# Loading the shifted tiles of a step in one transfer per tile over 128 partitions, in place of one per partition quadrant

## What is computed

```python
B, M, D = (2048, 32, 16)
e = jnp.stack([tbl_0[ids[:, 0]], ..., tbl_31[ids[:, 31]]], axis=1)   # x0: (B, 32, 16)
xk = x0
outs = []
for W in (W0, W1, W2):           # (32, 32, 64), (32, 64, 64), (32, 64, 64)
    xk = jax.nn.relu(jnp.einsum('bmd,bhd,mhk->bkd', x0, xk, W))
    outs.append(jnp.sum(xk, axis=2))
z = jnp.concatenate(outs, axis=1)                  # (B, 192)
h = jnp.concatenate([z, dense_ctx], axis=1)        # (B, 208)
h = jnp.maximum(h @ W_top1 + b_top1, 0.0)
h = jnp.maximum(h @ W_top2 + b_top2, 0.0)
y = h @ W_top3
```

## Time and profile before

| | |
|---|---|
| median of 3 runs | 1177.02 us |
| the profiled execution itself | 1183.16 us |
| its span, first to last instruction | 1181.4 us |
| mean granted TensorE clock | 0.993 |
| PE busy | 1126.9 us, 95% |
| DVE busy | 1119.0 us, 95% |
| POOL busy | 914.9 us, 77% |
| ACT busy | 822.8 us, 70% |
| DMA moved | 167.31 MB, mean 142 GB/s |
| queue 1 (SP's) | 59,248 packets, 157.76 MB, 61.3% of 16 engines |

### The profile page before, as it was taken

The page is one execution under the profiler, slowest core; times in us unless marked ns, Lnnn a source line. Parts: engine busy times, 40 slices in busy tenths (PEclk is TensorE's granted clock), DMA queues, the critical chain, the costliest instruction groups (busy, mean ns, idle before and its releaser), DMA issues.

```text
span 1181.4 us, 15688 instructions
## 1 busy us (share of the span) xinstructions
PE 1126.9 (95%) x5370; PEld 399.8 (34%) x5370; DVE 1119.0 (95%) x511; ACT 822.8 (70%) x2259; POOL 914.9 (77%) x639
## 2 busy tenths in 40 slices
PE   0778899999999999999999999999999999999998
PEld 0222223333333333333333333333333333333344
DVE  1689999999999999999999999999999999999995
ACT  0345466776869677686967768696776869678674
POOL 6766888888888888888888888888888888885400
PEclk9998999999999999999999999999999999999999
DMA  6786588666677866657886666688666678866300
GB/s 145 194 197 137 114 173 171 142 145 140 132 150 165 174 141 148 131 123 161 169 173 144 139 131 147 140 171 173 141 142 132 140 145 173 173 139 136 70 1 1
DMA packets 78336, 167.31 MB, mean 142 GB/s; under 512 B 22097, under 2 KB 39905, under 8 KB 78257
## 3 DMA queue, kind: packets, MB, share of 16 engines
q1 hardware_dynamic: 59248, 157.76, 61.3%
q0 software_dynamic: 16384, 4.23, 3.7%
q10 hardware_dynamic: 2624, 4.34, 1.4%
HBM read 157.86 MB, written 8.40 MB: 141 GB/s over the span
## 4 chain that ended last, share of the span: by engine, by line
PE 84%; POOL 4%; DMA 4%; DVE 3%; issue 3%; ACT 1%; ACTq 0%; SPq 0%; DVEq 0%; POOLq 0%
PE acc L758 79%; POOL x_rows L346 3%; PE acc L862 3%; DVE p_dve L653 2%; PE acc L848 1%; POOL p_l L359 1%; PE acc L850 1%; DMA spread<-x_of_steps 1%; DMA q_tile<-x_of_steps 1%; DMA x_of_steps<-x_rows 1%; PE acc L870 1%; DMA x_rows<-in_table,ids_s 0%; ACT xb L411 0%; POOL p_pool L370 0%; DVE z L680 0%
## 5 line engine op out<-in xcount | busy, mean ns | idle before, releaser
L758 PE MATMUL acc<-p_dve,w_s 128*64 128x512 f32 x3840 | 855.8, 595 | 13.9 <-DVE p_dve L653 13.7
L346 POOL DMA_INDIRECT x_rows<-in_table,ids_s x512 | 493.8, 964 | 146.1 <-issue 130.7
L653 DVE TENSOR_TENSOR p_dve<-spread,xb 128x3072 f32<-128x3072 f32 (+2 forms) x225 | 566.1, 2572 | 4.3 <-PE acc L758 2.9
L653 DVE TENSOR_TENSOR p_dve<-spread,xa 128x2048 f32<-128x2048 f32 (+1 forms) x192 | 495.4, 2634 | 9.3 <-PE acc L758 4.1
L758 PEld LDWEIGHTS acc<-p_dve,w_s 128*64 128x64 f32 x3840 | 271.3, 137 | 549.7 <-issue 486.5
L411 ACT ACTIVATE xb<-acc 32x512 f32<-32x512 f32 x512 | 288.8, 564 | 36.1 <-DVE p_dve L653 29.6
L359 POOL TENSOR_TENSOR p_l<-spread,q_tile 128x2048 f32<-128x2048 f32 x59 | 268.4, 4576 | 8.3 <-DMA q_tile<-x_of_steps 7.2
L402 ACT ACTIVATE xa<-acc 64x512 f32<-64x512 f32 x256 | 145.9, 570 | 168.5 <-PE acc L758 126.7
L370 POOL TENSOR_TENSOR p_pool<-spread,x_s 128x1024 f32<-128x1024 f32 x64 | 152.5, 2383 | 95.3 <-PE acc L758 52.8
L419 ACT ACTIVATE x_s<-acc 64x512 f32<-64x512 f32 x256 | 151.5, 592 | 9.2 <-ACT y_row L565 4.7
L758 PE MATMUL acc<-p_l,w_s 32*64 32x512 f32 (+1 forms) x600 | 144.2, 617 | 5.5 <-DVE p_l L706 3.2
(11 more groups left out here) (26 smaller groups left out, 246.2 us busy)
## 6 DMA issues: line engine op xcount, KB each, us to landing
spread<-x_of_steps SPq DMA_DIRECT2D x244, 512.0 KB, 16.9
q_tile<-x_of_steps SPq DMA_DIRECT2D x120, 128.0 KB
x_rows<-in_table,ids_s POOLq DMA_INDIRECT x512, 4.2
x_of_steps<-x_rows SPq DMA_DIRECT2D x60, 128.0 KB
spread<-x_of_steps ACTq DMA_DIRECT2D x4, 512.0 KB, 12.0
spread<-x_of_steps SPq DMA_DIRECT2D x6, 256.0 KB, 4.7
w_s<-in_w SPq DMA_DIRECT2D x2, 512.0 KB, 6.3
spread<-x_of_steps SPq DMA_DIRECT2D x8, 128.0 KB, 3.3
```

The source lines that it names most:

```text
L346: nc.gpsimd.indirect_dma_start(out=x_rows[:, s % 2, i * DIM:(i + 1) * DIM], out_offset=None, in_=table, in_offset=bass.IndirectOffsetOnAxi ...
L653: nc.vector.tensor_tensor(p_dve[:, to:to + n, :], spread[:, s % 3, tile:tile + n, :], over(x[:], n), ALU.mult).then_inc(dve_made, n)
L758: last = nc.tensor.matmul(halves(acc[b * K:(b + 1) * K, :]), w, of_block(prod, b), start=start, stop=stop)
```

## The change

`load_tiles_by` gets a second way, taken when all four quadrants are asked for, that is in `load_a` and `load_b` from step 2 on. It issues one transfer per tile, whose destination is all 128 partitions of that tile and whose source is a pattern of 4 x 32 x 1024: the outer dimension steps by one row (the four quadrants' shifts), the middle one by one row too (the 32 rows).

```diff
         def load_tiles_by(engine, s, first_tile, n, quads, signal):
 
+            if len(quads) == Q:
+
+                for i in range(first_tile, first_tile + n):
+                    first = scratch[s, Q * i + 1:Q * i + 2, :]
+                    src = bass.AP(first.tensor, first.offset, [[COLS, Q], [COLS, FIELDS], [1, COLS]])
+                    engine.dma_start(spread[:, s % 3, i, :], src).then_inc(signal, 16)
+                return
             for q in quads:
                 o = Q * first_tile + q + 1
                 first = scratch[s, o:o + 1, :]
```

## The result

The changed kernel takes 1600.53 us (median of four runs, 1599.1 to 1601.56), the kernel before 1177.66 in the same comparison: a ratio of 1.358, 95% interval 1.355 to 1.361. It is slower, by the mechanism forecast, but by 423 us and not by 956.

A forecast was written before the change was run, and what follows sets the result against it. PE's compute bound the kernel at 34.5 us a step; the DMA queue would become the bound. 78.8 + 61.2, plus 29 periods of 66.7, plus 62.6 gave 2137 of span; + 1.8 - 6.1 gave 2133 us, range 1520 to 2780.

The forecast's parts named there:

- Four engines: The 240 changed `spread` loads: each on 4 engines of 16, queue 1's packets falling by 2880; 85 in 100.
- The price of a tile on four engines: Each changed a or b load: 7.65 us a tile at 17.1 GB/s an engine, 61.2 us for eight.
- the middle row: Profile window 31 to 41 us, two queues writing all quadrants: 274 GB/s, 17.1 an engine, taken for the tile price.
- the fast end: First instants of the a loads, 401 GB/s: 25.1 GB/s an engine, 5.23 us a tile, 1551 us in all.
- The q loads, 2.2 us, and the gap, 3.3 us: Each step: unchanged q loads, plus an unhidden gap from the last b packet to the next a packet.
- The end, 62.6 us after the last b load: Step 31: compute left after b(31) lands, from the group with chunk 4 to the span's end, 62.6 us.
- The gather no longer is waited for: SP's queue each step: the gather wait vanishes, POOL's 28.6 us of work being far below the 66.7 us period.
- rival 3: Changed loads on 8 engines or a like middle: 3.83 us a tile, 36.1 a step, about 1215 us; 3 in 100.
- the 26.6 us of SP's idle time: SP's gather wait each step, 26.6 us, taken to hide any longer issue of the new loads.
- Rival 1: Changed loads on all 16 engines at the fast rate: 5.2 us saved early, 1172 us; 8 in 100.
- SP's issues at nothing: SP's queue: four new issues may take up to 1 us more, hidden by SP's idle time, so no cost.
- The clock: PE idle over 30 us each step: lower clock costed at nothing within steps, some us allowed in the last 62.6.

The follow-up runs named there:

- e1: Changed kernel with the 240 loads' source written 16 x 8 x 1024 in place of 4 x 32 x 1024: 1216.52 us, ratio 1.0015 to the kernel before.
- e2: Changed kernel with the loads' source written 8 x 16 x 1024 in place of 4 x 32 x 1024: 1397.0 us, ratio 1.151 to the kernel before.
- t1: Changed kernel with source 16 x 8 rows, reading other embedding table rows for each load instead of the stored rows: 1181.27 us, ratio 1.002.
- t4: Changed kernel, source still 4 x 32 rows, reading embedding table rows (four engines' rows 33 apart) instead of the stored rows: 1603.68 us, ratio 1.363.
- e4: Changed kernel with one transfer per tile and quadrant, source 4 x 8 rows, 960 transfers of 128 KB: 1577.21 us, ratio 1.299.
- e6: Changed kernel with the last four gathers of a step moved ahead of the products in POOL's queue: 1593.55 us, ratio 1.352.
- e8: The e2 kernel with the last four gathers of a step moved ahead of the products in POOL's queue: 1276.83 us, +98 us.
- t3: Changed kernel with source one run of 128 successive embedding table rows per load, to 128 partitions: 1177.61 us, ratio 1.000.
- e3: Changed kernel with only the a loads in the new form, the b loads by quadrants as before: 1736.95 us, ratio 1.429.
- e5: Changed kernel unedited, run again beside e6 and e8: 1597.33 us against 1179.17 for the kernel before.

## Why the prediction was right in kind and wrong in size

- **Four engines.** Right, and shown by e1 and e2: 56,368 packets against "about 56,370". That the smaller outermost count, here the source's, decides, which I chose without a row for it, holds for 4, 8 and 16. The rule of the Trainium skill ("DMA: Bandwidth & Descriptors", the section on why a DMA increments its semaphore by 16) gives the same three numbers.
- **The price of a tile on four engines, 7.65 us at 17.1 GB/s an engine.** This is the step that failed. Measured are 26 GB/s an engine, 5.0 us a tile, in the whole b set and most of the a set, and 74 GB/s for four, some 18 an engine, only in the first 8 us. I took the middle row since in it all quadrants are written at once; but it has 16 engines in them, and with four the lower rate gives way to the higher. t1 and t4 rule out the re-reading of the same rows as the reason of the lower rate, and e4 shows the start without it; why it lies at the destination is argued above and not shown. Eight tiles so take some 45 us (a from 758 to about 784, b some 20) in place of 61.2. The measured rate is close to the fast end that I had in hand, 5.23 us a tile and 1551 us: the right row was in the prediction and I chose another. With 48.8 us for the period in my own sum in place of 66.7, 29 x 17.9 = 519 us go, and 16 more for step 2's own tiles: 2133 - 535 = 1598, against 1600.53 measured. This puts in the measured period, so it tests the start and the end of the sum and not the price of a step. That the transfers alone give that period is what e6 shows: with the loop broken, the time stays within 4 us.
- **The q loads, 2.2 us, and the gap, 3.3 us.** Nearly right in sum: about 2 us more on the four engines (82 GB/s from 784 to 786), and some 4 us from 805, where the b rows end, to 809, where the a rows begin. What I did not see is that q is now complete only behind the a rows, which is what POOL waits for.
- **The end, 62.6 us after the last b load.** It fits: the stores of step 31 are at 1484.38, the last b rows move at 95 GB/s up to 1534, and from 1534 to 1536 there are 2 GB/s. So b(31) lands at about 1534, 64 us before 1598.0.
- **"The gather no longer is waited for."** Wrong, and the second step that failed: SP waits for it 17.9 us a step. I counted POOL's work and not what it waits for. In the change this is nearly hidden by the b loads (e6: 4 us). It is what made rival 3 wrong, whose 36.1 us a step would be +38 us: eight engines cost +183, of which 85 are the loop and the other 98 (e8) the low rate of eight engines. And the 26.6 us of SP's idle time were no cover for later a and q loads; they were the loop's other half.
- **Rival 1's gain** did not exist: 16 engines on 128 partitions run at 234 GB/s in e1 and not at 401, and where they do run near it, in t3, no gain shows. The 5.2 us forecast, 0.44%, lie outside t3's interval.
- **SP's issues at nothing.** SP is held up to 4.2 us an issue; I expected 0.7 at most. I take that holding for an effect of full queues, which no run tests. What it cost I could not separate.
- **The clock.** PE is busy 94 us longer at a mean clock of 0.87; it was costed at nothing, and PE has only 5% of the chain that ended last, which fits. No run tests it. PE's share is 76%, not 53%, with the shorter time and the lower clock.

## What to carry to other kernels

Write a load so that the outermost counts of both sides are multiples of 16, as 16, 32 and 128 are here; a leading 4 in the source sent the whole transfer through four engines, with all 128 partitions at the other side, and it shows in the closing packets of a transfer. When a transfer gets slower, look for the loop that it stands in before calling the idle time of its queue cover: follow who waits for it, and what that one issues next. And be wary of mixing transfers on few engines with transfers on all: in e3 the a and q loads took 37.1 us in place of 32.4.

## What the runs showed of the hardware that I had not expected

- An engine that loads rows of 4 KB into SBUF has two rates, about 23 to 26 GB/s and about 12 to 15, and which it gets depends on the shape of the transfer, the bytes and the 16 engines being the same: 205 GB/s in single quadrants, 234 with 16 x 8 rows over all partitions (e1), 367 to 398 with a flat run of 128 rows to the same partitions (t3). That it is a matter of where the other engines write at that moment is the reading that fits all runs, and is not shown.
- With four engines the lower rate lasts 8 us from the start of an a set and then is gone (74, then 105 GB/s); with eight it lasted through a whole step in e8 (132); with sixteen it never left in e1's step (234).
- Half a change can cost more than all of it: +523 (e3) against +418 us (e5), each beside the kernel before of its own comparison.
- A load rate of nearly twice the old one, in t3, is worth nothing measurable to this kernel (ratio 1.000, 0.997 to 1.003).
